# Whole jobs instead of half jobs between the units of an attention loop

## The chip, the cores and the metric

The kernel runs on one core of one Trainium2 chip. The metric is the device time of one launch in microseconds (us). One launch does everything: attention over 8 batches of 1024 tokens, then a mixture of 16 experts and a shared one over all 8192 tokens.

## The reference, cut to what matters

```python
x = x + _layernorm(attn(_layernorm(x)))      # x is (8, 1024, 256), float32
x = x + _layernorm(ffn(_layernorm(x)))

def attn(query):                             # 16 heads of 16
    q = _split_heads(query @ q_w.T + q_b, h) / scale
    k = _split_heads(query @ k_w.T + k_b, h)
    v = _split_heads(query @ v_w.T + v_b, h)
    scores = jnp.einsum('bhqd,bhkd->bhqk', q, k)
    attn = jax.nn.softmax(scores.astype(jnp.float32), axis=-1)
    ctx = jnp.einsum('bhqk,bhkd->bhqd', attn, v)
    return ctx.transpose(0, 2, 1, 3).reshape(b, s, d) @ out_w.T + out_b
```

`ffn` is the mixture of experts. It runs in a stage of its own (`expert_stage`) after all of attention and has no part in the change.

## The kernel before, in words

`attention_stage` writes out by hand, engine by engine, the order of all instructions. A batch is 8 steps; step `s` takes four heads (`q = s // 2`) and one half of the queries, 512 of them (`f = s % 2`). A step is 8 units, one for each chunk `kc` of 128 keys. A batch so has 64 units, `u` = 0 to 63, and `kc` is 0 in the units 0, 8, 16 and so on.

In each unit TensorE issues, in this order: two score tiles of the next unit (`st`, L302, into the three banks `st_bank`), a maxima tile (`smax`, L314, into the three banks `sm_bank`), P times V of this unit (`pv`, L324, into `o_bank`, four matmuls that the profile shows as eight), a maxima tile, a score tile, a maxima tile, a score tile, then a job if one is planned for this unit, and the fourth maxima tile. Scores have keys on the partitions; ScalarE takes the exponential of the four tiles (L511) as they come, and P times V waits for all four of its unit. A fourth score tile can only be written when the exponential of the tile three before it is done. The maxima tiles are the same products the other way round, for the step two later: VectorE reduces each to its row maximum (L578), and each of the three banks is free only after that reduction. So four tiles of each kind go through three banks in a unit. At the first unit of a step VectorE also combines the two halves of the maxima (L585), and ScalarE copies `o_bank` out (L501), for which the next step's first P times V waits.

The jobs are all the other TensorE work of attention, for this batch or the ones beside it. They are planned in the table `JOBS`: unit, kind, batch offset, number, part. `XT` transposes the normalised input (L340), `QK` projects it on Q or K for one half of the tokens and of the columns (L348, six matmuls of 512 columns), `V` projects two chunks on V (L357, twelve matmuls of 256 columns), `OP` is the output projection of two chunks (L379, twelve of 256), `CT`, `OT` and `SH` are transpositions (L370, L365, L361), `SH` of a 16-column tile. Each projection has three matmuls per product, since float32 values are split in a high and a low part. All jobs share the one bank `job_bank`: a job waits until the readers of the job before are done with it.

A `QK`, `V` or `OP` job can be cut in two: part 0 issues the first half of its matmuls in one unit, part 1 the second in the next unit, and only then is `job_ready` signalled. The readers come in the unit after that. ScalarE, after its four exponentials of that unit: for `QK` the high part with the bias (L467), for `V` a copy (L472), for `OP` a copy (L484). VectorE, at the start of the unit, for `QK` alone: the low part (L605), which waits for ScalarE's high part. `XT` and `CT` have such a low part too (L595, L605). VectorE's statistics for LayerNorm stand in fixed units: `X_STATS`, `A_STATS` (L538 to L552) and three small operations at the units in `SEEDS` (L555, L557, L560). SP loads the results of `QK` to `qk_stack` by DMA (`load_stack`) and GpSimd copies `v_stage` (L744) and adds the output bias (L738), each behind the readers.

The kernel does the first batch's `XT`, `QK` and `V` jobs whole before the loop; in the loop `QK` and `V` belong to the batch after, `OP` to the batch before, so each of these kinds runs in 7 of the 8 batches.

Of the kernel before, what the change touches and what calls it, by code (L numbers as in the profile page):

```python
# [39 lines left out]
JOBS = {  # L40
    0: ("CT", -1, 0, None), 3: ("CT", -1, 1, None), 11: ("CT", -1, 2, None), 12: ("CT", -1, 3, None),
    2: ("OT", -1, 7, None),
    23: ("XT", 1, 0, None), 24: ("XT", 1, 1, None), 27: ("XT", 1, 2, None), 28: ("XT", 1, 3, None),
}
# [2 lines left out]
    if _s:  # L47
        JOBS[8 * _s + 2] = ("OT", 0, _s - 1, None)
for _kind, _off, _i, _at in (
# [3 lines left out]
    for _n, _u in enumerate(_at):  # L53
        JOBS[_u] = (_kind, _off, _i + _n // 2, _n % 2)

X_STATS = {0: 0, 2: 1, 5: 2, 6: 3, 7: 4, 8: 5, 9: 6, 10: 7}
A_STATS = {14: (0, 0), 15: (0, 1), 17: (0, 2), 20: (0, 3), 30: (1, 0), 32: (1, 1), 36: (1, 2), 38: (1, 3)}
# [1362 lines left out]
```

## Time and profile before

| | us |
|---|---|
| median of 3 runs | 2961.0 (2960.58 to 2962.13) |
| the profiled execution | 2961.1 |
| its span, first to last instruction | 2959.3 |

| engine | busy in the span |
|---|---|
| TensorE, matmuls | 2805.3 us (95%) |
| VectorE | 2259.0 us (76%) |
| ScalarE | 1643.3 us (56%) |
| GpSimd | 541.0 us (18%) |

The attention loop ends near 1660 us of the span, the rest is the expert stage. In a batch of the loop (197.3 us) TensorE is busy for 98%, VectorE for 93% and ScalarE for 78% of the time. Matmuls are pipelined and the rows of neighbours overlap, so starts say more than durations; the same is true of VectorE and ScalarE, whose rows overlap by some 0.1 us. In a timeline a row merges neighbours of one kind; "x8" is their count and the second number the time from the first's start to the last's end.

### The profile page before, as it was taken

How to read it: one execution, taken by the hardware profiler on the slowest of the kernel's cores; microseconds unless marked ns; L12 is line 12 of the kernel's file. 1: busy time of each engine (PE TensorE's matmuls, PEld its weight loads, DVE VectorE, ACT ScalarE, POOL GpSimd, SP SyncE). 2: the span in 40 equal slices, each digit the busy share in tenths (PEclk: the TensorE clock that was granted, in tenths of full speed). 3: DMA queues.
4: the chain of work that ended last, by engine and by line, in shares of the span. 5: the costliest groups of instructions: out<-in, count | busy, mean ns of one | idle time of the engine just before them, and what ended most of it. 6: DMA issues, size and time to landing. Idle time of an engine off the chain costs nothing. (4 is left out here: it accounts for less than half of the span.)

```text
span 2959.3 us, 47558 instructions
## 1 busy us (share of the span) xinstructions
PE 2805.3 (95%) x16898; PEld 1718.8 (58%) x16898; DVE 2259.0 (76%) x4788; ACT 1643.3 (56%) x3095; POOL 541.0 (18%) x664
## 2 busy tenths in 40 slices
PE   5999999999999999999999659999999999999997
PEld 3434443443444434434443348888888888888886
DVE  5898999999989999999898146666666666666654
ACT  1577777777777777777777424333333333333332
POOL 4010220310312203103112220111111111111112
PEclk8899999999999999999999769999999999999999
DMA  5203332233133322330330033222322222232221
GB/s 91 44 17 50 44 73 38 51 51 52 31 58 45 73 37 51 52 51 17 57 44 23 22 110 108 79 79 79 78 78 79 80 79 79 78 78 79 79 72 54
DMA packets 120396, 180.59 MB, mean 61 GB/s; under 512 B 14160, under 2 KB 76768, under 8 KB 118112
## 3 DMA queue, kind: packets, MB, share of 16 engines
q1 hardware_dynamic: 120160, 177.55, 27.6%
q8 instruction: 135, 2.21, 0.3%
q14 instruction: 101, 0.83, 0.1%
HBM read 108.81 MB, written 17.30 MB: 43 GB/s over the span
## 5 line engine op out<-in xcount | busy, mean ns | idle before, releaser
L578 DVE TENSOR_REDUCE score_max<-sm_bank 128x1 f32<-128x512 f32 x2048 | 1305.2, 681 | 115.8 <-PE sm_bank L314 107.9
L511 ACT ACTIVATE probs<-st_bank 128x512 f32<-128x512 f32 x2048 | 1097.8, 598 | 346.8 <-PE st_bank L302 345.0
L314 PE MATMUL sm_bank<-qk_stack 64*128 64x512 f32 x2048 | 793.2, 462 | 21.6 <-DMA qk_stack<-qk_stack 10.6
L302 PE MATMUL st_bank<-qk_stack 64*128 64x512 f32 x2048 | 748.0, 449 | 21.7 <-ACT probs L511 20.8
L314 PEld LDWEIGHTS sm_bank<-qk_stack 64*128 64x128 f32 x2048 | 327.2, 187 | 574.8 <-DVE score_max L578 529.3
L324 PE MATMUL o_bank<-probs,v_quad 128*32 128x512 f32 x4096 | 545.4, 605 | 8.5 <-ACT o_sb L501 7.3
L1263 DVE TENSOR_TENSOR gated<-gate_act,u_bank 128x512 f32<-128x512 f32 x256 | 175.8, 687 | 311.1 <-ACT gate_act L1094 311.1
L1094 ACT ACTIVATE gate_act<-g_bank 128x512 f32<-128x512 f32 x272 | 162.5, 598 | 429.0 <-PE u_bank L1000 428.8
L302 PEld LDWEIGHTS st_bank<-qk_stack 64*128 64x128 f32 x2048 | 307.9, 184 | 72.3 <-ACT probs L511 49.3
L1105 ACT ACTIVATE h_hi<-h 128x512 fp32r<-128x512 f32 x272 | 172.0, 632 | 317.8 <-DVE h L1266 283.3
L1014 PE MATMUL y_bank<-f_w_hi,h_hi 128*128 128x256 f32 x1088 | 311.8, 287 | 5.9 <-DVE h_lo L1274 5.8
L1014 PE MATMUL y_bank<-f_w_hi,h_lo 128*128 128x256 f32 x1088 | 305.1, 280 | 0.0
L1014 PE MATMUL y_bank<-f_w_lo,h_hi 128*128 128x256 f32 x1088 | 303.7, 279 | 0.0
L1364 POOL TENSOR_SCALAR f_x_in<-f_x_in,f_mv,f_rstd 128x256 f32<-128x256 f32 x64 | 90.8, 1431 | 707.3 <-DVE f_rstd L1175 707.3
L1274 DVE TENSOR_TENSOR h_lo<-h,h_hi 128x512 fp32r<-128x512 f32 x272 | 185.5, 682 | 44.9 <-ACT h_hi L1105 41.6
L1000 PE MATMUL g_bank<-f_xT_lo,f_w_hi 128*128 128x512 f32 x544 | 216.7, 398 | 0.0
L1000 PE MATMUL g_bank<-f_xT_hi,f_w_hi 128*128 128x512 f32 x544 | 215.2, 396 | 1.5 <-DVE gated L1263 1.5
L1000 PE MATMUL g_bank<-f_xT_hi,f_w_lo 128*128 128x512 f32 x544 | 216.1, 397 | 0.0
L1000 PE MATMUL u_bank<-f_xT_hi,f_w_hi 128*128 128x512 f32 x544 | 215.8, 397 | 0.0
L1000 PE MATMUL u_bank<-f_xT_lo,f_w_hi 128*128 128x512 f32 x544 | 215.6, 396 | 0.0
L1000 PE MATMUL u_bank<-f_xT_hi,f_w_lo 128*128 128x512 f32 x544 | 215.4, 396 | 0.0
L1014 PEld LDWEIGHTS y_bank<-f_w_hi,h_hi 128*128 128x128 f32 x1088 | 205.3, 189 | 16.7 <-DVE h_lo L1274 6.5
(186 smaller groups left out, 3490.7 us busy)
## 6 DMA issues: line engine op xcount, KB each, us to landing
cb<-comb_dram SPq DMA_DIRECT2D x256, 256.0 KB, 3.7
qk_stack<-qk_parts SPq DMA_DIRECT2D x384, 128.0 KB
x_in<-in_x SPq DMA_DIRECT2D x8, 1024.0 KB, 6.4
x_res<-in_x SPq DMA_DIRECT2D x16, 512.0 KB, 3.8
x<-x_res SPq DMA_DIRECT2D x16, 512.0 KB, 2.9
f_x_in<-x SPq DMA_DIRECT2D x16, 512.0 KB, 3.9
f_x_res<-x SPq DMA_DIRECT2D x16, 512.0 KB, 7.1
out<-f_x_res SPq DMA_DIRECT2D x16, 512.0 KB, 3.2
```

Of the source, the lines that this page charges most:

```text
L302: mm(st_bank[tile % RING][:, :], k_stack[q][p][rows, kc * CH:(kc + 1) * CH], q_stack[q][p][rows, f * HALF:(f + 1) * HALF], start=True, sto ...
L314: mm(sm_bank[n % RING][:, :], q_stack[q][p][rows, tok:tok + CH], k_stack[q][p][rows, half * HALF:(half + 1) * HALF], start=True, stop=True ...
L324: last = mm(o_bank[32 * j:32 * j + 32, :], v_quad[q][:, kc, VW * j:VW * j + 32], probs[0 if kc % 2 == 0 else 1][:, j, :], start=(kc == 0), ...
L511: nc.scalar.activation(probs[kc % 2][:, j, :], st_bank[(4 * U + j) % RING][:, :], ACT.Exp).then_inc(exp_done, 1)
L578: v.reduce_max(score_max[f][:, HC * (2 * p + e) + c, half:half + 1], sm_bank[n % RING][:, :], AX_X).then_inc(smax_read, 1)
L1000: last = mm(bank[:, :], w[b][:, e, col + k * HID:col + (k + 1) * HID], xT[par][a][:, k, :], start=(t == 0), stop=(t == len(steps) - 1))
L1014: last = mm(y_bank[:, c, :], h[i][a][:, c * CH:(c + 1) * CH], w[b][:, e, 2 * D:3 * D], start=(e == 0 and t == 0 and c % 2 == 0), stop=(e = ...
L1094: a_(gate_act[i][:, :], g_bank[i][:, :], ACT.Silu).then_inc(S["silu_done"], 1)
L1105: a_(h[i][0][:, :], h32[i][:, :], ACT.Copy).then_inc(S["h_hi_done"], 1)
L1263: v.tensor_tensor(gated[:, :], gate_act[i][:, :], u_bank[i][:, :], ALU.mult).then_inc(S["gated_done"], 1)
L1274: v.tensor_tensor(h[i][1][:, :], h32[i][:, :], h[i][0][:, :].bitcast(F32), ALU.subtract).then_inc(S["h_ready"], 1)
L1364: gp.tensor_scalar(x_in[:, c, :], x_in[:, c, :], mv[:, c, 0:1], rstd[:, c:c + 1], ALU.subtract, ALU.mult).then_inc(S["f_x_normed"], 1)
```

## The change

The 32 planned halves of a batch become 16 whole jobs: every `OP`, `QK` and `V` job of the loop is planned once, whole, in the unit in which its first half was, and the unit of its second half has no job. Part `None` issues all its matmuls in one go.

```diff
 for _kind, _off, _i, _at in (
-        ("OP", -1, 0, (5, 6, 7, 8)), ("OP", -1, 2, (15, 16, 20, 21)),
-        ("QK", 1, 0, (29, 30, 31, 32, 35, 36, 37, 38)), ("V", 1, 0, (39, 40, 43, 44, 45, 46, 47, 48)),
-        ("QK", 1, 4, (51, 52, 53, 54, 55, 56, 59, 60))):
+        ("OP", -1, 0, (5, 7, 15, 20)), ("QK", 1, 0, (29, 31, 35, 37)), ("V", 1, 0, (39, 43, 45, 47)),
+        ("QK", 1, 4, (51, 53, 55, 59))):
     for _n, _u in enumerate(_at):
-        JOBS[_u] = (_kind, _off, _i + _n // 2, _n % 2)
+        JOBS[_u] = (_kind, _off, _i + _n, None)
```

No instruction is added or removed, and the order of the jobs among themselves stays. The units 6, 8, 16, 21, 30, 32, 36, 38, 40, 44, 46, 48, 52, 54, 56 and 60 are left without a job. The readers of each job come one unit sooner.

## Rows read from the trace of the kernel before

**Rows 1.** The page, busy time, share of the span and instructions of each engine:

```profile
PE 2805.3 (95%) x16898; PEld 1718.8 (58%) x16898; DVE 2259.0 (76%) x4788; ACT 1643.3 (56%) x3095; POOL 541.0 (18%) x664
```

**Rows 2.** The page, chain that ended last, shares of the span by line:

```profile
PE y_bank L1014 13%; PE u_bank L1000 12%; PE g_bank L1000 12%; PE f_job_bank L961 0%; PE f_job_bank L974 0%; POOL f_x_in L1364 0%; PE f_job_bank L984 0%; PE f_job_bank L976 0%; DMA f_w_raw<-in_w_down 0%; DVE f_w_lo L1157 0%; PE f_job_bank L971 0%; DMA f_x_in<-x 0%; POOL y L1371 0%; ACT x_sq L1074 0%; DVE gated L1263 0%
```

**Rows 3.** Windows, two batches: stretch, length, busy PE, PEld, DVE, ACT, POOL, clock, DMA:

```profile
493.38:690.64 197.26, 193.87 (x1240) 79.93 (x1240) 184.31 (x346) 153.38 (x289) 38.77 (x62) 1.00 0.29 50
690.64:887.92 197.28, 193.92 (x1241) 79.96 (x1241) 184.33 (x346) 153.39 (x289) 38.74 (x62) 1.00 0.29 50
```

**Rows 4.** Waits in the batch from 493.38: us in total, times, longest:

```profile
PEld sm_bank L314 <- DVE score_max L578: 66.3, 103, 0.8
...
ACT probs L511 <- PE st_bank L302: 43.4, 81, 0.9
```

**Rows 5.** Timeline of TensorE, unit 29, first half of a Q job: start, us, what:

```profile
581.74 1.07 PE L324 MATMUL o_bank<-probs,v_quad 128*32 128x512 f32 x8
...
583.40 0.50 PE L348 MATMUL job_bank<-xT_hi,wq_hi 128*128 128x512 f32 x1
583.74 0.39 PE L348 MATMUL job_bank<-xT_lo,wq_hi 128*128 128x512 f32 x1
583.97 0.40 PE L348 MATMUL job_bank<-xT_hi,wq_lo 128*128 128x512 f32 x1
584.30 0.49 PE L314 MATMUL sm_bank<-qk_stack 64*128 64x512 f32 x1
...
584.96 1.07 PE L324 MATMUL o_bank<-probs,v_quad 128*32 128x512 f32 x8
```

**Rows 6.** Timeline, unit 21, second half of an output projection:

```profile
559.66 0.39 PE L379 MATMUL job_bank<-wo_hi,cT_hi 128*128 128x256 f32 x1
...
559.88 0.28 PE L379 MATMUL job_bank<-wo_hi,cT_lo 128*128 128x256 f32 x1
...
560.35 0.28 PE L379 MATMUL job_bank<-wo_lo,cT_hi 128*128 128x256 f32 x1
...
560.56 0.50 PE L314 MATMUL sm_bank<-qk_stack 64*128 64x512 f32 x1
```

**Rows 7.** Timeline of all engines, unit 22, which has no job:

```profile
561.22 1.07 PE L324 MATMUL o_bank<-probs,v_quad 128*32 128x512 f32 x8
...
562.75 1.89 DVE L578 TENSOR_REDUCE score_max<-sm_bank 128x1 f32<-128x512 f32 x3 [0.27 <-PE sm_bank L314]
562.79 1.57 ACT L511 ACTIVATE probs<-st_bank 128x512 f32<-128x512 f32 x3 [0.54 <-PE st_bank L302]
...
563.53 0.47 PE L302 MATMUL st_bank<-qk_stack 64*128 64x512 f32 x1 [0.35 <-ACT probs L511]
...
563.97 0.64 PE L324 MATMUL o_bank<-probs,v_quad 128*32 128x512 f32 x4
```

**Rows 8.** Timelines of TensorE and VectorE, unit 61, no job, behind a K job:

```profile
681.15 0.50 PE L314 MATMUL sm_bank<-qk_stack 64*128 64x512 f32 x1
...
681.82 1.06 PE L324 MATMUL o_bank<-probs,v_quad 128*32 128x512 f32 x8
...
684.72 0.64 PE L324 MATMUL o_bank<-probs,v_quad 128*32 128x512 f32 x4
...
682.30 0.74 DVE L605 SCALAR_TENSOR_TENSOR qk_parts<-job_bank,bias,qk_parts 128x512 fp32r<-128x512 f32 x1
682.96 2.47 DVE L578 TENSOR_REDUCE score_max<-sm_bank 128x1 f32<-128x512 f32 x4
```

**Rows 9.** Timelines of TensorE and VectorE, start of a step, behind a transposition job:

```profile
566.21 0.49 PE L314 MATMUL sm_bank<-qk_stack 64*128 64x512 f32 x1
...
567.63 0.69 DVE L595 TENSOR_TENSOR xT_lo<-job_bank,xT_hi 128x512 fp32r<-128x512 f32 x1
```

**Rows 10.** Timeline of VectorE, unit 21, first and last of three small operations:

```profile
560.14 0.16 DVE L555 TENSOR_SCALAR var_a<-mv_a 128x4 f32<-128x4 f32 x1
...
560.53 0.17 DVE L560 TENSOR_SCALAR rstd_a<-rstd_a 128x4 int32<-128x4 int32 x1
```

## The prediction

> **What bounds the kernel now.** I read the page first, then the waits of one batch, then the timeline of single units. TensorE is busy for 95% of the span [rows 1], and in the chain that ended last TensorE has every large share [rows 2], but those shares lie in the expert stage (its lines are those of g_bank, u_bank and y_bank), which the change doesn't touch. The attention loop must be read by itself. From the third batch's start at 493.38 us a batch of 64 units lasts 197.26 us and the next one 197.28 [rows 3]: the loop repeats to the hundredth, so a cost found once in a batch counts for each. In it TensorE's queue waits 66.3 us for VectorE's reading of the maxima banks, in 103 places, and ScalarE 43.4 us for scores [rows 4]. No engine is the bound everywhere; it changes from unit to unit. So I measure a unit, always from the first P times V matmul of one unit to that of the next.
>
> Where a unit holds half a projection, TensorE is the bound. The unit of rows 5 runs from 581.74 to 584.96, 3.22 us, of which the half job takes 583.40 to 584.30, 0.90 us; nothing in it waits. Without the job TensorE has 2.32 us of work in a unit. Half an output projection costs the same: 559.66 to 560.56, 0.90 us [rows 6].
>
> Where a unit holds no job, TensorE is not the bound. The unit of rows 7 runs from 561.22 to 563.97, 2.75 us, though TensorE has only 2.32 us to do. What ends last are two chains that tie. VectorE: the unit's second maxima tile is issued about 1.0 us after the unit's start and its reduction starts at 562.75, 1.53 in; it ends 0.70 later; only then is its bank free for the first maxima tile of the next unit, which goes out at 563.53 (three banks, four tiles in a unit), and P times V follows 0.44 later. ScalarE: the exponentials of the last two score tiles start at 562.79 and end 1.08 later, at 563.87, and P times V waits for them, 0.10 more: 563.97 too. A unit without a job therefore has a floor of 2.75 us, and 0.43 us of TensorE time in it is unused. That gap is what half jobs fill.
>
> **The change part by part.** It removes nothing and adds no instruction, wait or DMA. Of the 16 jobs in a batch that were split (4 output projections, 8 Q/K, 4 V) the second half moves from its own unit into the unit of the first half. Hence 16 pairs of two 3.22 us units become 16 pairs of one longer unit and one without a job. The last batch has no Q/K and V jobs and the first has no output projections, so each kind counts for 7 batches.
>
> The longer unit. A further Q/K matmul starts 0.23 us after the one before, 583.74 to 583.97 [rows 5]; I take 0.22, since the first one pays something extra, so three more are 0.66. A V or output-projection matmul of 256 columns adds (560.35 - 559.88) / 4 = 0.118 [rows 6], six more 0.71. No row shows a whole job behind 64-row tiles; 0.21 and 0.24 for Q/K, and 0.70 to 0.75 for the others, are my ends.
>
> The unit without job, V and output projection: VectorE has no work on the result, and ScalarE's copy lies before the score tiles that the floor is made of; the unit of rows 7 stands behind such a job and has that copy in it. So 2.75. Each pair: 3.22 + 0.71 + 2.75 = 6.68 against 6.44, +0.24; eight of them in a batch, +1.92 us.
>
> The unit without job, Q/K: the result is read by ScalarE and then by VectorE ahead of the next reductions. One such unit exists today, behind the last Q/K job [rows 8]. Count from 681.15, TensorE's first matmul behind the job. Once ScalarE has read the job's bank and VectorE has ended its pending reduction, VectorE starts on the low part at +1.15, and the four reductions start at +1.81, so that the second starts at +2.41 (reductions in a row start 0.60 apart: four take 2.47, the last of them 0.68); its tile would be there at +0.66 + 1.53 = +2.19 [rows 5, 7]; P times V comes at 684.72, +3.57, a unit of 2.90. Each pair: 3.22 + 0.66 + 2.90 = 6.78, +0.34. For six of the eight jobs that holds: +2.04.
>
> Two of the eight (units 31/32 and 55/56) have their empty unit at the start of a step, where VectorE also combines the maxima first. Behind a transposition job there the low part starts at 567.63 against 566.21 for the first matmul behind the job, so +1.42 in place of +1.15 [rows 9]. With 0.27 more the unit is 3.17 and the pair 7.05, +0.61: together +1.22. For V and output projections the combine costs nothing: the first reduction behind it starts at about +1.42, where the low part starts in rows 9, and the second at +2.02, still before +2.19. That cover is 0.17 us; if it is gone, these four units cost up to 0.27 each.
>
> What comes later. The low part is now done one unit earlier, and the units 33, 57 and 61 lose it: unit 61 goes from 2.90 to 2.75, and the other two hold only a small transposition, so I credit 0.45 in all. Against it, VectorE runs with little slack out of an empty unit that also holds three small operations on the row statistics (units 16, 21, 40): they start 0.19 to 0.20 us apart, 560.14 to 560.53 [rows 10], about 0.48 in the row of reductions. In such a unit the second reduction starts at +2.19, the third at +2.19 + 0.60 + 0.48 = +3.27, the next unit's second three further, at +5.07, where its tile is there at 3.41 + 1.53 = +4.94: 0.13 late, and 0.05 more behind a job as short as the gap. LayerNorm statistics in unit 8 do the same, less. I take 0.6 us for the four units.
>
> Queues passed. Jobs end one unit sooner, so the DMAs that wait for them (SP's stacks behind Q/K 3 and 7) and GpSimd's copies and bias additions are released some 3 us sooner; their order isn't touched, and none of them ends a wait of TensorE in rows 4. I take zero, and bound it by 0.8 us in a batch either way, the longest single wait there.
>
> Sum per batch: 1.92 + 2.04 + 1.22 - 0.45 + 0.60 = 5.33 us; by 7 batches 37.3 us. The profiled execution was 2961.1 us and the median 2961.0, so one base serves: 2998 us, +1.3%. Against it stands a rule. The Trainium skill, TensorEngine Tiling (Array Packing), Key Properties, says that a change of tiling mode drains TensorE. The trace agrees in kind: the first matmul of the half job holds its place for 0.34 us and the next for 0.23 [rows 5], so whole jobs do spare entries; the sum has this in it, since only further matmuls are charged. By that rule alone the change would be a gain, which is the first rival.
>
> **The rivals.** First, faster: the banks are elastic enough for TensorE to run ahead in the empty units. Then a whole Q/K job costs 0.90 + 0.66 instead of 1.80, 0.24 us saved, and the others 1.61 instead of 1.80, 0.19 saved: (8 x 0.24 + 8 x 0.19) x 7 = 24 us, 2937 us. It decides at an empty unit of 3.22 - 0.71 = 2.51 us or 3.22 - 0.66 = 2.56: shorter, and the change gains. For it speaks that 2.32 is all TensorE has to do; against it that the unit of rows 7 takes 2.75 although the unit before it left VectorE and ScalarE idle. 6%. The Trainium skill, Perfetto Trace Analysis, Identifying Performance Opportunities, reads a gap that repeats as too few buffers, which is how I read rows 7; it speaks against this rival.
>
> Second, the floor alone: the Q/K results are read beside the wait and the late statistics cost nothing. All 16 empty units take 2.75: (8 x 0.24 + 8 x 0.19) x 7 = 24 us, 2985 us. Rows 8 speak against it. 12%.
>
> Third, dearer: VectorE carries its lateness out of every empty unit, 0.15 us each: 16 x 7 x 0.15 = 17 us more, 3015 us. Against it: a whole-job unit of 3.9 us asks only 2.4 us of reductions of VectorE, which wipes out any arrears. 9%.
>
> Fourth, the change doesn't do what it says: the weight loads or the bank's reader space the second half out, or the empty units are filled by something else, and the time stays at 2961. All operands are there before the job starts. 3%.
>
> **How the numbers follow.** My forecast, 2998, has 70%. Its own bounds: without the 0.60 it is 2994 and with the low matmul ends 2992; with the 0.27 for four combines and no credit for the three units it is 3009. The range takes in the second rival: 2983 to 3010. Under 0.2% (6 us) this kernel's measurement can't tell a change from none. Faster 6%, same 3%, slower 91%.
>
> **What would show each step.** A batch in the steady loop should last 202.6 us instead of 197.3. A Q/K unit of 3.88 us should be followed by one of 2.90 (3.17 at a step's start), a V or output-projection unit of 3.93 by one of 2.75. In the empty units the first maxima tile of the next unit should go out some 0.08 us after a reduction ends, and TensorE's wait for VectorE should grow. The totals of matmuls, exponentials and reductions stay. The expert stage keeps its time and the granted clock its 1.00 of rows 3. An empty unit under 2.5 us would prove the sum wrong in sign; one over 3.0 behind V jobs would prove it too small.

## The result, and the profile after

The changed kernel takes 2998.0 us (median of 4 runs, 2997.5 to 2999.1) against 2961.1 before: 1.0125 times as long, 95% interval 1.0107 to 1.0142. The forecast was 2998, inside 2983 to 3010. The profiled execution took 2998.25 us.

The windows view of two steady batches, with the columns of [rows 3]:

```profile
502.50:705.27 202.77, 195.71 (x1241) 83.94 (x1241) 183.76 (x346) 152.07 (x289) 38.70 (x62) 1.00 0.28 48
705.27:907.98 202.71, 195.65 (x1241) 83.92 (x1241) 183.72 (x346) 152.04 (x289) 38.69 (x62) 1.00 0.29 48
```

A batch lasts 202.7 to 202.8 us where it lasted 197.3, with the same instructions on every engine and the clock at full. From the attention loop's last P times V matmul to the end of the span it is 1297.7 us, 1298.8 before. All of the loss is in the loop: it takes 38.2 us longer, and 1.1 us come back behind it.

The waits view of one batch (us in total, times, longest), to set against [rows 4]:

```profile
PEld sm_bank L313 <- DVE score_max L577: 70.4, 108, 0.9
...
ACT probs L510 <- PE st_bank L301: 41.9, 71, 0.9
...
DVE score_max L577 <- PE sm_bank L313: 18.0, 36, 1.0
```

The weight loads' wait for VectorE hardly moves: 70.4 us against 66.3. It sums the time for which weight loads stand still, and most of it passes while earlier matmuls run (they are busy for 193.9 of the 197.3 us before, for 195.7 of the 202.8 now), so it doesn't price the change. The single units do. TensorE's timeline through V job 1, whole in unit 43, and the empty unit 44:

```profile
638.10 1.06 PE L323 MATMUL o_bank<-probs,v_quad 128*32 128x512 f32 x8
...
639.76 0.39 PE L356 MATMUL job_bank<-wv_hi,xT_hi 128*128 128x256 f32 x1
639.99 0.28 PE L356 MATMUL job_bank<-wv_hi,xT_lo 128*128 128x256 f32 x1
...
641.12 0.28 PE L356 MATMUL job_bank<-wv_lo,xT_hi 128*128 128x256 f32 x1
641.33 0.49 PE L313 MATMUL sm_bank<-qk_stack 64*128 64x512 f32 x1
...
641.99 1.07 PE L323 MATMUL o_bank<-probs,v_quad 128*32 128x512 f32 x8
...
644.20 0.49 PE L301 MATMUL st_bank<-qk_stack 64*128 64x512 f32 x1 [0.25 <-ACT probs L510]
644.27 0.49 PE L313 MATMUL sm_bank<-qk_stack 64*128 64x512 f32 x1
644.69 1.06 PE L323 MATMUL o_bank<-probs,v_quad 128*32 128x512 f32 x8
```

The unit with the job takes 3.89 us, the one without 2.70. In the second, TensorE stands still before 644.20, as it did in [rows 7], for a bank that a reader still holds. The timelines of TensorE and VectorE at the last K job, unit 59, and the empty unit 60, to set against [rows 8]:

```profile
689.83 1.07 PE L323 MATMUL o_bank<-probs,v_quad 128*32 128x512 f32 x8
...
691.49 0.50 PE L347 MATMUL job_bank<-xT_hi,wk_hi 128*128 128x512 f32 x1
...
692.75 0.40 PE L347 MATMUL job_bank<-xT_hi,wk_lo 128*128 128x512 f32 x1
693.07 0.49 PE L313 MATMUL sm_bank<-qk_stack 64*128 64x512 f32 x1
...
693.74 1.07 PE L323 MATMUL o_bank<-probs,v_quad 128*32 128x512 f32 x8
...
696.63 0.64 PE L323 MATMUL o_bank<-probs,v_quad 128*32 128x512 f32 x4
...
694.21 0.74 DVE L604 SCALAR_TENSOR_TENSOR qk_parts<-job_bank,bias,qk_parts 128x512 fp32r<-128x512 f32 x1
694.87 2.47 DVE L577 TENSOR_REDUCE score_max<-sm_bank 128x1 f32<-128x512 f32 x4
```

3.91 and 2.89 us. Behind the job's end at 693.07 the low part starts at +1.14, the four reductions at +1.80, and P times V comes at +3.56: the spacing of [rows 8] to 0.01 us.

One unit is far from the forecast. Unit 8, empty behind an output projection, takes 3.21 us instead of 2.75. The timelines of TensorE, VectorE and GpSimd there:

```profile
528.39 1.07 PE L323 MATMUL o_bank<-probs,v_quad 128*32 128x512 f32 x8
...
530.58 0.50 PE L313 MATMUL sm_bank<-qk_stack 64*128 64x512 f32 x1 [0.46 <-DVE score_max L577]
...
531.60 0.64 PE L323 MATMUL o_bank<-probs,v_quad 128*32 128x512 f32 x4
...
528.99 0.94 DVE L584 TENSOR_TENSOR row_max<-score_max 128x16 f32<-128x16 f32 x1
529.85 0.68 DVE L577 TENSOR_REDUCE score_max<-sm_bank 128x1 f32<-128x512 f32 x1
...
528.61 1.28 POOL L737 TENSOR_TENSOR attn_out<-attn_out,out_bias 128x512 f32<-128x512 f32 x1 [5.38 <-ACT attn_out L483]
```

VectorE's combine of the maxima takes 0.94 us, where all eight in a batch of the kernel before took 0.17 to 0.18. It ends at 529.93, just behind GpSimd's bias addition, which runs from 528.61 to 529.89. The reductions behind it start so much later, and TensorE waits for one of them. Two more of the eight combines are longer than before, those of the units 24 (0.33 us) and 48 (0.37 us), each beside a GpSimd instruction; unit 48, empty too, takes 2.70 us all the same.

### The profile page after: what moved, and what is told of

The parts are those of the page before. It is cut to its first block and busy times, and to the rows that moved or that the text cites. A ratio compares the mean times of both kernels' runs of the same rounds, so it can differ in the third digit from the quotient of the medians.

```text
span 2996.4 us, 47558 instructions
## 1 busy us (share of the span) xinstructions
PE 2816.8 (94%) x16898; PEld 1746.0 (58%) x16898; DVE 2255.5 (75%) x4788; ACT 1633.7 (55%) x3095; POOL 540.5 (18%) x664
## 5 line engine op out<-in xcount | busy, mean ns | idle before, releaser
L313 PE MATMUL sm_bank<-qk_stack 64*128 64x512 f32 x2048 | 812.1, 466 | 36.1 <-DVE score_max L577 17.7
L313 PEld LDWEIGHTS sm_bank<-qk_stack 64*128 64x128 f32 x2048 | 336.6, 187 | 601.7 <-DVE score_max L577 557.9
L301 PEld LDWEIGHTS st_bank<-qk_stack 64*128 64x128 f32 x2048 | 317.6, 184 | 109.6 <-ACT probs L510 76.1
```

The costliest lines, as they stand in the source:

```text
L301: mm(st_bank[tile % RING][:, :], k_stack[q][p][rows, kc * CH:(kc + 1) * CH], q_stack[q][p][rows, f * HALF:(f + 1) * HALF], start=True, sto ...
L313: mm(sm_bank[n % RING][:, :], q_stack[q][p][rows, tok:tok + CH], k_stack[q][p][rows, half * HALF:(half + 1) * HALF], start=True, stop=True ...
```

## The experiments

The theory is that of the prediction, called the floor: a unit without a job can't be shorter than some 2.7 us, since four tiles go through three banks and P times V waits for the exponentials, and TensorE loses 0.4 us in it. Its rival is the long block: VectorE and ScalarE starve while TensorE works on one long job, and the loss grows with the block. Unit lengths below are from P times V to P times V, means over the six middle batches.

**Uneven parts.** Each split job keeps its two units, five sixths of its matmuls in the first, one sixth in the second. (The job's matmuls are put in one list and sliced, and readers wait for the slice that ends the list; nothing else differs.)

```diff
-        JOBS[_u] = (_kind, _off, _i + _n // 2, _n % 2)
+        JOBS[_u] = (_kind, _off, _i + _n // 2, ((0, 5), (5, 6))[_n % 2])
```

> Every split job of the kernel before keeps its two units, but five sixths of its matmuls stand in the first and one sixth in the second. Theory of the floor (a unit without a job costs some 0.4 us of TensorE that it can't use): the second unit holds 0.90 - 0.46 = 0.44 us of job, just what fills that gap, so it takes 2.76 us and the first 3.22 + 0.46 = 3.68, together 6.44 as with halves: 2961 us, at most 3 more. Rival, the long block (VectorE and ScalarE starve while TensorE works on one long job, and the loss grows with the block): the block is 1.36 us instead of 0.90, two thirds of the way to a whole job, so some 25 of the 37 us come: 2985 us.

Measured: 2967.8 us, ratio 1.0028 (1.0017 to 1.0039). TensorE's timeline through units 43 and 44:

```profile
627.44 1.06 PE L324 MATMUL o_bank<-probs,v_quad 128*32 128x512 f32 x8
...
631.10 1.07 PE L324 MATMUL o_bank<-probs,v_quad 128*32 128x512 f32 x8
632.76 0.39 PE L355 MATMUL job_bank<-wv_hi,xT_lo 128*128 128x256 f32 x1
632.99 0.28 PE L355 MATMUL job_bank<-wv_lo,xT_hi 128*128 128x256 f32 x1
...
633.87 1.06 PE L324 MATMUL o_bank<-probs,v_quad 128*32 128x512 f32 x8
```

3.66 and 2.77, 6.43 together: two matmuls in the second unit are enough to give back all that the whole job loses there, though the long block is nearly as long as a whole job. The rival's 2985 didn't come. Nor was it 2961: a batch is 1.4 us longer than with halves. That lies for the most part in units I hadn't stepped through. In the short second unit VectorE no longer catches up before its low part of a Q/K job, which is due at the start of the unit after. So unit 33 takes 3.39 us (2.96 before), the units 57 and 61 0.09 more each than before, and the units 31, 37 and 39, whose jobs need the bank that the low part still reads, 0.11 more each than the 3.68 of the others. Behind the short units with statistics VectorE is late too: 9, 17, 22 and 41 take 0.31 us more together.

**One kind at a time.** Only the Q/K jobs, only the V jobs, only the output projections whole:

```diff
-        JOBS[_u] = (_kind, _off, _i + _n // 2, _n % 2)
+        JOBS[_u] = (_kind, _off, _i + _n, None) if _kind in ('QK',) else (_kind, _off, _i + _n // 2, _n % 2)
```

with the units of the changed kernel for the kind named, and in the other two runs `('V',)` and `('OP',)`.

> Only the Q/K jobs whole, V and output projections in halves. From the unit lengths of the changed kernel: six pairs at +0.37, two at the start of a step at +0.59, less 0.55 in the units 33, 57 and 61: +2.85 us in a batch, by 7 batches 20 us: 2981 us. If the kinds act on each other the three runs of one kind don't add up to the 37 us of all.

> Only the V jobs whole. Four pairs at 0.19 on average and 0.16 in unit 41: 0.93 us in a batch, 6.5 us in all: 2967.5 us. Unit 48, which combines the maxima without a job on VectorE, stays at 2.70 us.

> Only the output projections whole. Three pairs at 0.20, 0.70 in the pair of units 7 and 8, and 0.43 in the units 9, 17, 22 and 25: 1.73 us in a batch, 12 us in all: 2973 us. If the long combine of maxima in unit 8 (0.94 us) comes from GpSimd's bias addition beside it, it is here too; if it came from Q/K or V, unit 8 is back at 2.75 us and the time at 2970.

Measured: 2979.7, 2966.9 and 2972.9 us, ratios 1.0067 (1.0052 to 1.0082), 1.0023 (1.0014 to 1.0032) and 1.0040 (1.0026 to 1.0054) to 2960.1 in the same runs. In their traces a batch is 2.86, 0.94 and 1.76 us longer than before, 5.56 together, against 5.52 for all of them at once. The kinds don't act on each other by more than 0.04 us, and the price comes pair by pair.

**Short reads: does the sign turn?** VectorE's reductions and ScalarE's exponentials read 192 of 512 columns; TensorE does the same work. The other 320 columns take no part in the maxima and the weights, so these kernels leave out a part of the attention and serve for their times alone. Once on the kernel before, once on the changed one. (`probs[1]` is filled with ones once at the start.)

```diff
-                    v.reduce_max(score_max[f][:, HC * (2 * p + e) + c, half:half + 1], sm_bank[n % RING][:, :],
+                    v.reduce_max(score_max[f][:, HC * (2 * p + e) + c, half:half + 1], sm_bank[n % RING][:, 0:192],
...
-                        nc.scalar.activation(probs[kc % 2][:, j, :], st_bank[(4 * U + j) % RING][:, :],
+                        nc.scalar.activation(probs[kc % 2][:, j, 0:192], st_bank[(4 * U + j) % RING][:, 0:192],
```

> The kernel before, in which VectorE's reductions of the maxima and ScalarE's exponentials read 192 of their 512 columns (the rest of each row takes no part in maxima and weights); TensorE's work stays. Theory of the floor: the two chains behind the second tile of a unit get some 0.3 us shorter each, so units without a job fall from 2.75 to below 2.5 us, and those with a half job stay at 3.22. With about 8 such units and the waits around transpositions some 4 us in a batch go: 2930 us.

> The changed kernel with the same short reads. Theory of the floor: once a unit without a job takes less than 2.51 us, whole jobs gain what they spare at entries, 0.19 to 0.24 us each: 24 us below the kernel before with short reads, 2906 us, so the sign turns. Rival, the long block, where the loss comes from the length of the job: VectorE and ScalarE have even less to do during it, and this kernel stays above the other by most of 37 us.

Measured: 2872.4 and 2860.3 us (2871.5 to 2873.1, and 2859.6 to 2860.6). With short reads the whole jobs are 12.1 us faster; with full reads they are 37 us slower. Unit 44 of the changed kernel with short reads:

```profile
587.54 1.06 PE L323 MATMUL o_bank<-probs,v_quad 128*32 128x512 f32 x8
589.91 1.07 PE L323 MATMUL o_bank<-probs,v_quad 128*32 128x512 f32 x8
```

2.37 us, below the 2.51 at which the prediction let the sign turn; the units with a whole job stay at 3.90 to 3.94. Two sizes were off. The gain is half of the 24 us, since the empty units come down to 2.37 or 2.47 (unit 8 to 2.55) and not to 2.32, and a Q/K job's second half adds 0.69 and not 0.66. And the kernel before gained 88 us from short reads where I expected 31: a batch fell by 7.9 us, not 4, as units with transpositions waited for the readers as well; the first and the last batch, which have more units without a job, fell by 11 and 17 us, and another 13 us went ahead of the loop, where the first two steps' maxima are read.

**Which reader holds the floor.** The changed kernel with short reads on VectorE alone, and on ScalarE alone, by the same edits.

> The changed kernel with short reads (192 of 512 columns) in VectorE's reductions alone. Two chains tie in an empty unit, so ScalarE's keeps V's empty units at 2.70 and those behind Q/K jobs fall from 2.90 and 3.11 to about 2.73: 1.9 us in a batch, with unit 8 and VectorE's lateness some 3 us: about 2977 us. If VectorE's chain were the only one, the V units would fall below 2.5 as with both reads short, and the time towards 2860.

> The changed kernel with short reads in ScalarE's exponentials alone. VectorE's chain keeps V's empty units at 2.70 or more and those behind Q/K jobs at 2.90; only the last unit of a step without a job, which waits for ScalarE's copy, gets shorter: 2990 us. If ScalarE's chain were the only one, the V units would fall below 2.5.

Unit 44 on TensorE's timeline, first with VectorE's short reads, then with ScalarE's:

```profile
614.60 1.07 PE L323 MATMUL o_bank<-probs,v_quad 128*32 128x512 f32 x8
...
617.30 1.06 PE L323 MATMUL o_bank<-probs,v_quad 128*32 128x512 f32 x8
```

```profile
638.83 1.06 PE L323 MATMUL o_bank<-probs,v_quad 128*32 128x512 f32 x8
...
641.52 1.07 PE L323 MATMUL o_bank<-probs,v_quad 128*32 128x512 f32 x8
```

2.70 and 2.69: either reader alone keeps the floor, and only both together let it go to 2.37. The units behind Q/K jobs fall from 2.90 and 3.11 to 2.70 to 2.74 with VectorE's short reads and stay with ScalarE's, so there it is VectorE alone. The totals are 2943.5 us (expected 2977) and 2986.1 (expected 2990). The first is low since VectorE's reads also end the waits in units 1, 4, 11, 13, 19 and others that have nothing to do with the change: a batch is 6.1 us shorter than the changed kernel's, and 12.6 us went ahead of the loop.

**The low part later.** VectorE does the low part of a Q/K job behind the unit's second reduction:

```diff
-                        if part != 0:
+                        if kind != "QK":
                             job(kind, b + off, i)
                     if maxima:
                         reduce(S + 2, (s + 2) % STEPS, kc, 0)
+                    if u - 1 in JOBS and not skipped(JOBS[u - 1], first, last) and JOBS[u - 1][0] == "QK":
+                        job("QK", b + 1, JOBS[u - 1][2])
```

> The changed kernel with VectorE's low part of a Q/K job behind the unit's second reduction instead of ahead of the first. If the low part ahead of the reductions is what lifts the empty units behind Q/K jobs from 2.75 to 2.90 and 3.11, they fall to about 2.75: 6 x 0.17 + 2 x 0.36 = 1.7 us in a batch, less 0.2 in unit 33: 2987 us. Rival: VectorE's work is only moved and the next unit pays: 2998 us.

Measured: 3008.3 us, ten more than the changed kernel instead of eleven less. The empty units did what was expected, 2.90 and 3.11 down to 2.70 to 2.73. The next unit paid more than they gained: unit 31 takes 4.47 us instead of 3.91, 37 and 39 as much, 33 3.44 instead of 2.78, and 53, 55, 57 and 61 take 0.2 to 0.35 more each. A batch is 1.55 us longer than the changed kernel's. The timelines of TensorE and VectorE in unit 31:

```profile
601.37 1.06 PE L323 MATMUL o_bank<-probs,v_quad 128*32 128x512 f32 x8
602.49 0.49 PE L313 MATMUL sm_bank<-qk_stack 64*128 64x512 f32 x1
...
603.09 0.49 PE L313 MATMUL sm_bank<-qk_stack 64*128 64x512 f32 x1
...
603.59 0.51 PE L347 MATMUL job_bank<-xT_hi,wk_hi 128*128 128x512 f32 x1
...
601.43 0.42 DVE L547 BATCH_NORM_STATS2 stats_a<-attn_out 128x6 f32<-128x256 f32 x1
601.76 1.27 DVE L577 TENSOR_REDUCE score_max<-sm_bank 128x1 f32<-128x512 f32 x2
```

The two reductions left over from the empty unit run from 601.76 to 603.03, behind the low part and a statistic. TensorE's next two maxima tiles need their banks and go out 0.60 us apart instead of 0.34, and the job stands behind them in TensorE's order. I had said that a whole-job unit wipes out any arrears of VectorE. It does so only for what comes during the job; ahead of it the three banks bite at once.

**The bias addition later.** GpSimd's second addition of the first half also waits for the combine in unit 8:

```diff
                 for h in range(2):
+                    if f == 0 and h == 1 and B < BATCHES - 1:
+                        wait_apart(pool, row_max_ready, nth("SH", B + 1, 2), passed["pool"])
                     wait_apart(pool, job_read["OP"], nth("OP", B, 2 * f + h), passed["pool"])
```

> The changed kernel, in which GpSimd's second bias addition of the first half also waits until VectorE has combined the maxima in unit 8. If the addition holds the combine, which then takes 0.18 us again, unit 8 falls from 3.21 to 2.75: 0.46 x 7 = 3.2 us less, 2994.8 us. Rival: the combine is long for another reason, and the time stays at 2998.

Measured: 2995.2 us (2994.1 to 2995.5) against the changed kernel's 2998.0. VectorE's and GpSimd's timelines:

```profile
528.79 0.17 DVE L584 TENSOR_TENSOR row_max<-score_max 128x16 f32<-128x16 f32 x1
...
529.24 1.28 POOL L739 TENSOR_TENSOR attn_out<-attn_out,out_bias 128x512 f32<-128x512 f32 x1 [6.23 <-DVE row_max L584]
```

The combine takes 0.17 us again and unit 8 takes 2.71: the collision was the cause, and a batch is 0.5 us shorter, as forecast. The totals alone, 2.9 us apart, wouldn't show it; the two traces do.

**A version that beats both.** If an empty unit has 0.4 us to give away, the split should go further where units are empty already:

```diff
-        JOBS[_u] = (_kind, _off, _i + _n // 2, _n % 2)
+        JOBS[_u] = (_kind, _off, _i + _n // 2, ((0, 3), (3, 6))[_n % 2])
+for _kind, _off, _i, _at in (("OP", -1, 2, (14, 15, 16)), ("OP", -1, 3, (20, 21, 22)), ("QK", 1, 7, (60, 61, 62))):
+    for _n, _u in enumerate(_at):
+        JOBS[_u] = (_kind, _off, _i, (2 * _n, 2 * _n + 2))
+JOBS[59] = ("QK", 1, 7, (0, 1))
+JOBS[60] = ("QK", 1, 7, (1, 2))
```

> The kernel before with three more jobs reaching into units that have none: output projection 2 in thirds over the units 14, 15 and 16, number 3 over 20, 21 and 22, and the last K job over 59 to 62 (1, 1, 2 and 2 matmuls). By the floor theory a unit without a job has 0.4 us of TensorE to give away and an entry costs about 0.2. Units 14 to 16 take 9.18 us now and 3 x 2.32 + 3 x 0.19 + 1.42 = 8.95 then, units 20 to 22 as much less, units 59 to 63 take 15.25 now and 14.75 then: 0.97 us in a batch, 6.8 us in all: 2954 us. Rival: a split into more parts only adds entries, and it is 2961 or more.

Measured: 2955.4 us (median of 11 runs) against 2960.9, ratio 0.9983 (0.9974 to 0.9992). The windows view of its third batch:

```profile
491.79:688.39 196.60, 194.53 (x1241) 79.69 (x1241) 184.53 (x346) 153.35 (x289) 38.70 (x62) 1.00 0.29 50
```

No run of the one kernel is as long as the shortest of the other (2957.3 and 2958.2), and a batch is 0.66 us shorter, not 0.97. Units 20 to 22 gain 0.23 as forecast, and 59 to 63 gain 0.47 of 0.50. Units 14 to 16 gain nothing of their 0.23: unit 15 is the last of its step and takes 3.20 with a third of the job as with half (3.22), since the next P times V waits for ScalarE's copy of `o_bank`, as it does behind unit 63, which has no job at all (3.19).

## Why the prediction was right, and where it was wrong

Per batch, in us; measured are the differences between the two traces, unit by unit, as means over the six middle batches:

| term | forecast | measured |
|---|---|---|
| 8 pairs, V and output projection | +1.92 | +2.04 |
| 6 pairs, Q/K | +2.04 | +2.24 |
| 2 pairs, Q/K at a step's start | +1.22 | +1.18 |
| units 33, 57, 61 without the low part | -0.45 | -0.56 |
| VectorE late into units 9, 17, 22, 41 | +0.60 | +0.53 |
| not foreseen (unit 25 most of it) | 0 | +0.09 |
| sum | +5.33 | +5.52 |
| whole kernel | 37.3 | 38.2 in the loop, 37.1 in the span |

- *What bounds.* Right. The bound changes from unit to unit, a unit without a job has a floor, and the tie of two chains in it, read from one stretch of 2.75 us, is what the two runs with one short reader show.
- *The longer unit.* 3.93 for V and output projections was right (3.90 to 3.93). Q/K was mis-sized: further matmuls start 0.23 us apart, so three add 0.69 and not the 0.66 I took against the row I had. By six pairs that is 0.18 of the 0.20 in the second line.
- *The empty unit behind V and output projections.* Right in kind and a little long: 2.70 to 2.74. With unit 8 at the forecast 2.75 the eight pairs would be 1.58, not 1.92; at the 2.71 that it takes without the collision, 1.53. What hides this is unit 8, 0.46 dearer than forecast.
- *Unit 8: the step that failed.* The prediction named a cover of 0.17 us for the combine and a price of 0.27 if it was gone; it took the combine at its length in the trace of before. It also said that GpSimd's work is released sooner and took zero for it. It is released right onto the combine, which grows from 0.17 to 0.94 us. The bound of 0.8 us in a batch held it (0.46), the value taken didn't. Unit 25 is longer for what looks like the same reason: the combine ahead of it takes 0.33 us beside another GpSimd instruction. No run moved that one away, but the two go together: in the runs with full reads unit 25 takes 2.98 to 2.99 us wherever this combine takes 0.30 to 0.35 (the changed kernel, uneven parts, output projections whole, low part later, bias addition later), and 2.92 wherever it takes 0.18 (the kernel before, Q/K whole, V whole, the last version).
- *The empty unit behind Q/K.* Right to 0.01 us at 2.90, and 3.11 against 3.17 at a step's start.
- *The rivals.* The first, faster, has the right deciding point: with an empty unit of 2.37 us the sign turned. The third, that VectorE carries its lateness on, was dismissed with a reason that is only half true, as the run with the late low part showed; in this change itself it comes only as the 0.53 of the fifth line, since the low part stands ahead of the reductions.
- *The total.* The median grew by 36.9 us, forecast were 37.3, and that this is so close is partly luck. In a batch 0.34 too much in the floor, against 0.20 and 0.46 too little in the Q/K pairs and unit 8 and 0.13 too much in the other lines, leave the sum 0.19 too low, and the loop grew by 38.2 us, 0.9 more than forecast. The 1.1 us behind the loop, which the change doesn't touch, take that back; in the other runs this part of the span takes from 1297 to 1300 us as well.

## What to carry to other kernels

When engines exchange tiles through a few banks, filler work costs its length minus the gap of the unit it stands in; cut it so that no unit is left with an unused gap, and join it only where the readers' chain is shorter than the fast engine's own work. Find that chain by stepping one unit without filler from tile to reader to freed bank, and look for a second one that ties. And when a step is moved, lay the instructions it releases on other engines beside what runs there, as two engines that never met before may now hold each other up.

## What the runs showed of the hardware

VectorE's small combine of two SBUF operands (128x16) takes 0.17 us alone and waits to the end of a GpSimd addition of two SBUF operands that began before it: 0.94 us, ending 0.03 us behind it, in all seven batches that have one. With VectorE's short reads it began 0.05 us after the addition, took 1.27 us and ended 0.03 us behind it too. The Trainium skill, SBUF — State Buffer, SBUF: two separate sides, says that the pair of ports is held for a whole instruction and the other side fully blocks; the trace agrees here. It agrees for GpSimd's copy of `v_stage` (L743, 0.64 us), which reads one tensor: the combine in unit 48 that began 0.30 us after it took 0.37 us and ended 0.03 us behind it. It agrees less for another GpSimd instruction with one tensor operand, the normalisation of `attn_out` (L750, 1.22 us each). A combine that began 0.25 us after one ended 0.64 us before that one's row did, having taken 0.33 us, and in the kernel before a combine that began 0.65 us after the start of such a row took its plain 0.17. What in these rows is the hold of the ports stays open. The reductions, which read PSUM, show no growth: their mean over the whole run is 0.681 us before and 0.680 after.
